# Chunks of hy that begin three elements into rows of 1028 in a selective-state kernel with a quantised side branch

## The reference, cut to what matters

```python
xn = layernorm(x)                                   # (4, 1024, 256)
# block 1, d_inner = 512
x_inner, z = split(xn @ W_in.T, 2)
x_conv = silu(causal_conv(x_inner, taps=4) + conv_b)
s_C = (x_conv @ W_x.T)[..., 16:]
h[t] = 0.95 * h[t-1] + x_conv[t]                    # along the sequence
y = h * (s_C @ exp(B_log).T) * silu(z)
a = layernorm(xn + y @ W_out.T) * ln_g + ln_b
# block 2
f = dequant(quant(xn)) @ dequant(quant(weight)).T + bias
out = x + a + f
```

## Time and profile before

| what | value |
|---|---|
| median of 3 runs | 272.79 us (272.72 to 274.57) |
| span of the profiled execution | 272.2 us |
| PE busy | 217.7 us, 80% |
| DVE busy | 236.1 us, 87% |
| ACT busy | 157.8 us, 58% |
| POOL busy | 198.4 us, 73% |
| gates on POOL | 16, 49.6 us |
| tap 0 on POOL | 16, 46.2 us |
| low parts on POOL | 11, 27.0 us |
| POOL idle before tap 0, waiting for DVE's taps (L986) | 14.9 us |

### The profile page before, as it was taken

How to read it: one execution, slowest core, us unless ns; L and a number is a source line. 1 busy time by engine, 2 the same in 40 slices (tenths; PEclk the granted TensorE clock), 3 DMA queues, 4 the chain that set the end, 5 groups by cost and what they waited for, 6 DMA issues and landing times.

```text
span 272.2 us, 3762 instructions
## 1 busy us (share of the span) xinstructions
PE 217.7 (80%) x1252; PEld 180.9 (66%) x1252; DVE 236.1 (87%) x353; ACT 157.8 (58%) x240; POOL 198.4 (73%) x127
## 2 busy tenths in 40 slices
PE   0469959789999997786999895896999988459940
PEld 0348836467898965775898763785989667359930
DVE  4799999989998999689699999689999978785374
ACT  2797773567953456858755355759737263733540
POOL 1428999999568788986586979985697959943142
PEclk9999995979999999999799999999999999959995
DMA  7963000000000000013202000000202000001204
GB/s 234 291 189 125 1 2 0 1 0 0 2 0 1 2 0 1 2 37 117 78 2 77 0 0 0 0 0 0 77 0 77 2 0 0 0 17 64 77 0 154
DMA packets 10773, 11.12 MB, mean 41 GB/s; under 512 B 648, under 2 KB 10120, under 8 KB 10760
## 3 DMA queue, kind: packets, MB, share of 16 engines
q1 hardware_dynamic: 9488, 9.96, 11.1%
q10 hardware_dynamic: 1272, 0.99, 1.3%
HBM read 6.76 MB, written 4.19 MB: 40 GB/s over the span
## 4 chain that ended last, share of the span: by engine, by line
DVE 32%; PE 31%; issue 16%; ACT 11%; POOL 5%; DMA 2%; DVEq 1%; ACTq 0%; POOLq 0%; SPq 0%
DVE hy L1015 6%; DVE xc L986 4%; DVE nmu L1060 4%; PE slot L747 4%; PE slot L749 4%; PE slot L748 4%; PE obank L839 3%; PE obank L838 3%; PE obank L846 3%; DVE hy L1028 3%; POOL hy L407 2%; ACT xn L586 2%; PE obank L749 2%; PE obank L747 2%; PE obank L748 2%
## 5 line engine op out<-in xcount | busy, mean ns | idle before, releaser
L747 PE MATMUL slot<-xn_hi,w_in_lo 128*128 128x512 f32 x128 | 54.9, 429 | 10.2 <-DVE xd_lo L981 4.1
L399 POOL TENSOR_TENSOR xc<-xc,tap 128x1021 f32<-128x1021 f32 x16 | 46.2, 2887 | 14.9 <-DVE xc L986 14.9
L407 POOL TENSOR_TENSOR hy<-hy,sz 128x1024 f32<-128x1024 f32 x16 | 49.6, 3099 | 6.5 <-ACT sz L630 6.5
L749 PE MATMUL slot<-xn_hi,w_in_hi 128*128 128x512 f32 x128 | 53.2, 416 | 0.0
L748 PE MATMUL slot<-xn_lo,w_in_hi 128*128 128x512 f32 x128 | 53.2, 416 | 0.0
L1015 DVE TENSOR_TENSOR_SCAN hy<-decay,xc 128x1024 f32<-128x1024 f32 x16 | 44.0, 2756 | 0.0
L986 DVE SCALAR_TENSOR_TENSOR xc<-slot,cw,xc 128x1023 f32<-128x1023 f32 (+1 forms) x32 | 40.2, 1264 | 2.3 <-ACT tap L623 1.8
L747 PEld LDWEIGHTS slot<-xn_hi,w_in_lo 128*128 128x128 f32 x128 | 25.7, 201 | 21.5 <-DVE xd_lo L981 5.2
L839 PE MATMUL obank<-w_out_hi,y_hi 128*128 128x256 f32 x128 | 32.8, 287 | 0.0
L838 PE MATMUL obank<-w_out_lo,y_hi 128*128 128x256 f32 x128 | 32.6, 285 | 0.0
L749 PEld LDWEIGHTS slot<-xn_hi,w_in_hi 128*128 128x128 f32 x128 | 25.7, 200 | 6.4
(11 more groups left out here) (109 smaller groups left out, 543.0 us busy)
## 6 DMA issues: line engine op xcount, KB each, us to landing
y<-fx SPq DMA_DIRECT2D x7, 512.0 KB, 2.9
x_in<-L_attn_x SPq DMA_DIRECT2D x3, 1024.0 KB, 5.6
x_in<-L_attn_x SPq DMA_DIRECT2D x2, 512.0 KB, 4.1
rs<-L_attn_W_in SPq DMA_DIRECT2D x2, 512.0 KB, 8.9
fx<-L_attn_W_out SPq DMA_DIRECT2D x1, 512.0 KB, 11.7
y<-fx SPq DMA_DIRECT2D x2, 256.0 KB, 2.1
fx<-L_ffn_weight ACTq DMA_DIRECT2D x1, 256.0 KB, 6.8
xc<-L_attn_B_log ACTq DMA_DIRECT2D x1, 256.0 KB
```

Source lines behind the costliest of these rows:

```text
L399: pool.tensor_tensor(xc[:, c, TAPS - 1:], xc[:, c, TAPS - 1:], tap0[:, c % 2, 0:n], ALU.add).then_inc(conv_ready, 1)
L407: pool.tensor_tensor(hy[:, c, :], hy[:, c, :], sz[:, :], ALU.mult).then_inc(hsz_ready, 1)
L747: pe.matmul(dst, w_lo, m_hi, start=first, stop=False)
L749: return pe.matmul(dst, w_hi, m_hi, start=False, stop=last)
```

## The change

`hy` is no longer an array of its own. An array `hy_rows` with 1028 elements a row is allocated in its place, and `hy` is the view of elements 3 to 1026 of each row. Every use of `hy` is as before. Chunk c then begins 1028c + 3 elements into the array; `sz`, `y_hi`, `y_lo` and `xc` stay as they were.

```diff
         sz = sb("sz", [P, SEQ])
-        hy = sb("hy", [P, NCH, SEQ])
+        hy_rows = sb("hy_rows", [P, NCH, SEQ + TAPS])
+        hy = hy_rows[:, :, TAPS - 1:TAPS - 1 + SEQ]
         y_hi = sb("y_hi", [P, NCH, SEQ], F32R)
```

## The result

The changed kernel took 266.81 us (median of 4 runs, 266.06 to 267.92); the kernel before, run beside it, 273.53. The ratio is **0.974, with a 95% interval of 0.970 to 0.979**. The profiled execution has a span of 266.1 us, 6.1 less than the 272.2 of the earlier trace rows. In every run on record the time is 1.8 to 1.9 us above the span, so these two spans belong to times of about 274 and of 267.9: the profiled execution after is the longest of its four, and the medians lie 6.7 us apart.

What follows compares the result with a forecast made beforehand. No engine was full: DVE, busiest at 87%, and POOL block one another. Batch savings of 0.70 + 3.50 + 1.70 = 5.9 us gave a 266.3 span and 266.9 us forecast; 8-in-10 range 265.0 to 271.8.

Steps and rivals of the forecast that it cites:

- Price of an instruction: GpSimd gates and low parts: 2.00 us each, like tap 0 with its offset inputs, saving 0.35 us each.
- theory 1: General form of the predicted offset, in the follow-ups: gates and low parts quicken to 2.00 us when their inputs start unequally.
- The floor of two inputs: Skill's rule for GpSimd: shared read port, about 2.5 cycles an element wherever inputs begin; by it saving 0, time 272.8.
- Only the gates gain: Rival: output against second input matters, so low parts stay at 2.36 us; 3.1 us saved, time 269.7; chance 0.12.
- Offset has to be 12 bytes: Rival: only chunk 0 gains, its gate hidden, low part 0 in three batches worth 1.05; time 271.7; chance 0.06.
- No effect: Rival: tap 0 is quicker for another reason, or the two-input floor holds; time 272.8; chance 0.11.
- Slower: Rival: DVE and ACT pay for hy off alignment; at 0.4 us per DVE pass, 3.7 slower, 276.5; chance 0.06.
- Batches 1 and 2: Gates 1 and 2 save 0.35 us each and three low parts 1.05: 1.75 a batch, 3.50 together.
- Batch 3: Gates 1, 2 and 3 save 0.35, 0.30 and 0.35 us, two POOL low parts 0.70: 1.70.
- Batch 0: Gates 1 and 2 save 0.35 us each, passed on through products and PE; low parts worth nothing: 0.70.
- the clock: PE's granted clock: 1.2 us lost in one batch might go or strike batch 2 too; unsummed, 1.5 either side.
- 0.6 above the span: Median run time 272.79 exceeds the profiled span of 272.2 by 0.6 us, added to 266.3 to forecast 266.9.

Runs made afterwards that it cites:

- e1: Kernel before the change with only sz begun at element 3 of its row, hy and y_hi as before; ratio 0.995 (0.990 to 0.999).
- e3: Kernel before the change with sz and y_hi both begun at element 3, hy kept aligned; ratio 1.001 (0.996 to 1.007).
- The separate halves: Two runs on the kernel before: sz from element 13 (gates only), 271.54 us, 0.989; y_hi from element 1 (low parts only), 270.13 us, 0.985.
- e8: Kernel before the change with hy begun at element 3 but chunks still 1024 elements apart; 266.17 us, 0.975 (0.969 to 0.981).

## Why the prediction was right, and where only by luck

- **Price of an instruction.** 2.00 us was forecast, 1.99 measured, by tap 0's row. Its reason held only in part: not any unequal start, but a first input 8 or 12 bytes ahead modulo 16. With sz or y_hi shifted by the same 3 elements the same reasoning forecast 0.989, 0.990 and 0.974 to 0.979 (theory 1 in the expectations of e1 to e3), and nothing came. That the change had the sign of the one row that the forecast rested on is what made it come out.
- **The floor of two inputs.** The Trainium skill (GPSIMD Engine Reference, section Architecture) puts it at approximately 2.5 cycles an element and names no condition on where the inputs begin. The runs show no single cost: the same operation on the same 1024 elements takes 2.35 or 1.99 us. If the aligned rate of 2.14 ns an element is the page's 2.5 cycles, the quick instructions, at no more than 1.95 ns an element with their start included, lie under that floor (an estimate).
- **Rivals.** "Only the gates gain", for which output against second input decided, falls with the low parts' 1988 ns: their output y_lo and their second input y_hi begin alike. "Offset has to be 12 bytes" falls with the changed kernel's gates 2 and 3 and its three low parts in 5.92 us. "No effect" falls with both. "Slower" by DVE and ACT off alignment: scans, products and y_hi are unchanged.
- **The path.** Batches 1 and 2 were forecast at 1.75 each, 0.70 for gates and 1.05 for low parts. Measured: gates 0.81 and 0.78, low parts 1.17 and 1.18, since what the path gains is nearer 0.39 than 0.35 an instruction (7.10 less 5.92 for three). Batch 3: 1.70 forecast, 1.75 measured; ve beside gate 2 lost its wait as forecast (0.45 to 0.16). nmr kept its 1.76, and gate 3 stayed hidden: POOL's wait for y_hi behind it grew from 1.07 to 1.40. The test that the prediction set itself, xd_lo in batch 1 at least 1.4 us earlier within its step, is met: 127.16 became 124.94, 2.22 earlier, less the 0.24 that the step began with.
- **Batch 0 and the clock** are where the sum was off. Batch 0 was forecast at 0.70, and 0.24 was left at the next gate 1: the saving was there at 56.06 and went when PE ran at a granted clock of 0.62 from 60 to 64. The prediction let PE follow the products and pass the saving on; PE did follow them 0.97 us earlier, but its transposes then took 3.6 us instead of 2.0. The clock's loss in batch 1, left as it was in the sum, went away (1.00), and 0.89 was given back at the end, after the long idle time before the last output tiles.
- **Luck.** Less 0.46 in batch 0, plus 1.00, less 0.89: these three nearly cancel. The forecast of 266.9 also started from 272.79, the median of three runs; beside the changed kernel the one before took 273.53, so 5.9 us were forecast (a ratio of 0.978) and 6.7 measured (0.974). The closeness of 266.9 to 266.81 is chance to that extent. So is the "0.6 above the span": the runs show 1.8 to 1.9, and the profiled execution before was one of the longer ones. The term drops out of the difference.
- **The separate halves** confirm the accounting: 3.1 us forecast for the gates, 2.7 measured in medians; 2.8 for the low parts, 4.1 measured, with a clock and a start-up that helped. The single terms of their traces (above) are closer than these totals.

What stays open: why 8 and 12 are quick and 0 and 4 slow. Differences that aren't multiples of 4, other operations and inputs of other element sizes weren't tried; `dequantise`, with one input of one byte an element, takes 1.91 to 1.92 us (medians) for 1024 elements in all of the traces. Nor is it settled what decides whether PE's clock falls after a wait. In e8's execution one of the 40 slices in batch 0 stands at 0.5, where the changed kernel has two at 0.7, and its transposes have the full clock.

## What to carry to other kernels

When a GpSimd instruction has two float32 inputs in on-chip memory, look at the difference of their start addresses (first less second) modulo 16 and make it 8 or 12, by three spare elements before the first input or one before the second: here each such instruction took 15% less. It is worth something only where another engine waits for GpSimd or is blocked beside it, so count those places in the ordered view first. And when a forecast rests on one row that happens to have the property, change each side of the pair in turn before calling the property by its name.

## What the runs showed of the hardware

- A two-input GpSimd instruction over 1024 float32 elements (tap 0: 1021) that nothing blocks takes 2.34 to 2.44 us with a difference of 0 or 4 modulo 16 bytes and 1.98 to 2.01 with 8 or 12; add, multiply and subtract alike, with the second input broadcast over four tiles too (scale_g).
- DVE's subtraction of the same kind of pair shows no such effect: the low part on DVE is 1208 ns at least before and 1207 after.
- A POOL instruction blocked by a DVE scan keeps its own duration behind it: gate 1 went from 4.37 to 3.98, by the 0.39 that a low part in a row of three gained as well.
- After 2.04 to 2.11 us without work PE's clock was at the low level in 7 of 16 cases, after 0.90 to 0.93 us in none of 10.
